# First weights issued after the images, position table and its five products moved behind the patch work

## The reference

```python
patches = x.reshape(B, C, h, P, w, P).transpose(0, 2, 4, 3, 5, 1).reshape(B, h * w, P * P * C)
y = _layernorm(patches, ln1_w, ln1_b)
y = jnp.einsum('bnp,pd->bnd', y, lin_w) + lin_b
y = _layernorm(y, ln2_w, ln2_b)
cls = jnp.broadcast_to(cls_token, (B, 1, y.shape[-1]))
y = jnp.concatenate([cls, y], axis=1)
y = y + pos_embedding[:, :n + 1]
```

## Time and profile before

| | |
|---|---|
| median of 3 runs | 350.81 us (349.03 to 353.78) |
| profiled execution, its own time | 349.38 us |
| its span, first to last instruction | 347.6 us |
| PE busy | 264.2 us (76%) |
| DVE busy | 221.0 us (64%) |
| ACT busy | 113.9 us (33%) |
| POOL busy | 75.7 us (22%) |
| DMA moved | 12.10 MB |

### The profile page before, as it was taken

The page is one execution under the profiler, slowest core; times in us unless marked ns, Lnnn a source line. Parts: engine busy times, 40 slices in busy tenths (PEclk is TensorE's granted clock), DMA queues, the critical chain, the costliest instruction groups (busy, mean ns, idle before and its releaser), DMA issues.

```text
span 347.6 us, 5644 instructions
## 1 busy us (share of the span) xinstructions
PE 264.2 (76%) x2202; PEld 215.6 (62%) x2202; DVE 221.0 (64%) x493; ACT 113.9 (33%) x249; POOL 75.7 (22%) x114
## 2 busy tenths in 40 slices
PE   2078986986695999999996877777585799707397
PEld 2067875986684578777785657556474576407385
DVE  0785577218646488979881258958847346898851
ACT  0034031202421510111133957466231244975000
POOL 5140022012502000000012197929201000333000
PEclk9999995965698999999999999999898599956789
DMA  7930008930000000000000000000000000000001
GB/s 185 298 51 23 2 0 305 307 119 2 2 2 1 2 0 2 0 0 0 3 0 0 3 0 3 2 0 2 3 0 2 0 0 2 0 0 1 0 26 46
DMA packets 16148, 12.10 MB, mean 35 GB/s; under 512 B 4603, under 2 KB 15578, under 8 KB 16122
## 3 DMA queue, kind: packets, MB, share of 16 engines
q1 hardware_dynamic: 13864, 10.01, 10.4%
q10 hardware_dynamic: 2258, 1.73, 1.5%
HBM read 11.13 MB, written 0.61 MB: 34 GB/s over the span
## 4 chain that ended last, share of the span: by engine, by line
PE 50%; DVE 20%; POOL 13%; ACT 7%; DMA 5%; issue 4%; ACTq 0%; DVEq 0%; POOLq 0%
PE bank L1425 37%; POOL big L548 11%; DMA sqr<-in_L_tok_ln_b 5%; DVE part L1318 3%; PE bank L1515 3%; PE bank L1693 2%; PE bank L1420 2%; PE bank L1497 2%; POOL rstd L523 2%; PE bank L1560 2%; DVE big L1381 1%; DVE st L902 1%; PE bank L1577 1%; PE bank L1546 1%; ACT big L635 1%
## 5 line engine op out<-in xcount | busy, mean ns | idle before, releaser
L1425 PE MATMUL bank<-xT,big 128*128 128x296 f32 x160 | 41.4, 413 | 0.0
L1425 PEld LDWEIGHTS bank<-xT,big 128*128 128x128 f32 x160 | 30.3, 190 | 9.2
L548 POOL TENSOR_SCALAR big<-keys_n,k_w 128x256 f32<-128x256 f32 x40 | 30.0, 768 | 23.0 <-DVE keys_n L1047 13.9
L1420 PE MATMUL bank<-ident,ones 128*128 128x128 f32 x128 | 22.9, 353 | 6.3 <-POOL queries_n L516 6.3
L1425 PE MATMUL bank<-xT,fT 128*128 128x296 f32 x96 | 26.0, 431 | 0.3 <-ACT xT L657 0.3
L1318 DVE TENSOR_REDUCE part<-big 128x1 f32<-128x296 f32 (+1 forms) x30 | 18.2, 641 | 12.7 <-ACT big L840 12.5
L1420 PEld LDWEIGHTS bank<-ident,ones 128*128 128x128 f32 x128 | 21.4, 260 | 7.2 <-POOL queries_n L516 6.3
L1425 PE MATMUL bank<-big,cur 128*128 128x256 f32 (+1 forms) x100 | 23.3, 381 | 0.7 <-DVE cur L1159 0.7
L746 ACT ACTIVATE cen<-bank 128x296 f32<-128x296 f32 x20 | 8.3, 417 | 46.4 <-PE bank L1425 40.7
L1425 PEld LDWEIGHTS bank<-xT,fT 128*128 128x128 f32 x96 | 18.9, 200 | 6.6 <-issue 0.8
L523 POOL TENSOR_TENSOR rstd<-var,nhalf 128x5 f32<-128x5 f32 (+3 forms) x7 | 6.8, 976 | 71.8 <-DVE var L913 34.3
(11 more groups left out here) (265 smaller groups left out, 565.6 us busy)
## 6 DMA issues: line engine op xcount, KB each, us to landing
big<-in_x SPq DMA_DIRECT2D x3, 576.0 KB, 9.2
big<-in_L_ffn_w_gate SPq DMA_DIRECT2D x2, 512.0 KB, 9.6
big<-in_L_ffn_w_up SPq DMA_DIRECT2D x2, 512.0 KB, 9.2
big<-in_L_ffn_w_down SPq DMA_DIRECT2D x1, 1024.0 KB, 8.5
big<-in_L_tok_lin_w SPq DMA_DIRECT2D x3, 256.0 KB, 9.5
small<-in_L_ffn_w_gate SPq DMA_DIRECT2D x1, 768.0 KB, 4.6
small<-in_L_ffn_w_up SPq DMA_DIRECT2D x1, 768.0 KB, 6.6
small<-in_L_ffn_w_down SPq DMA_DIRECT2D x1, 768.0 KB, 7.9
```

Source lines behind the costliest of these rows:

```text
L548: ins = pool.tensor_scalar(dst[:, :, n, :], src, scale[:, n:n + 1], by, ALU.mult, ALU.mult)
L1420: pe.matmul(b[:, 0:P], ones[:, :], ident[:, :], start=True, stop=True)
L1425: ins = pe.matmul(out_, a_, b_, start=(n == 0), stop=(n == len(pairs) - 1))
```

## The change

Three moves. On ACT the fourteen weight DMAs wait until all three images have landed. On DVE `make_table` runs behind the normalised patches and no longer between the variance and the wait for the inverse root. On PE, in the list of banks and on ACT, the five `ad` tiles come after the twelve `xp` tiles, and the four dummy products that stood ahead of them are gone.

```diff
@@ fills()
-    for t in range(TT):
-        f.append((("ad", t), "act"))
     for g in range(2):
         for k in range(6):
             f.append((("xp", k, g), "act" if k % 2 else "dve"))
+    for t in range(TT):
+        f.append((("ad", t), "act"))
@@ act
+            for c in range(NC):
+                act.wait_ge(images_in[c], 16)
             for name, arg in (("q0", "L0_attn_Wq"), ("o0", "L0_attn_Wo"), ("q1", "L1_attn_Wq"),
...
-            for t in range(TT):
-                n = P if t < TT - 1 else LAST
-                b = take(act, ("ad", t))
-                empty(act.copy(addend[0:n, t, :], b[0:n, 0:D + 1]))
             act.wait_ge(cols_in, 16 * N_COLS)
...  (the odd xp tiles)
+            for t in range(TT):
+                n = P if t < TT - 1 else LAST
+                b = take(act, ("ad", t))
+                empty(act.copy(addend[0:n, t, :], b[0:n, 0:D + 1]))
@@ dve
-            variance_given(dve.tensor_scalar(var[0:96, 0:NG], mv[0:96, :, 1], EPS, None, ALU.add), make_table)
+            variance_given(dve.tensor_scalar(var[0:96, 0:NG], mv[0:96, :, 1], EPS, None, ALU.add))
...  (normalised patches)
-            dve.wait_ge(consts_ready, N_CONSTS)
+            make_table()
@@ pe
-            for t in range(TT):
-                rows = P if t < TT - 1 else LAST
-                b = fill(("ad", t))
-                if t == 0:
-                    keep_awake(b, 4)
-                    pe.wait_ge(table_ready, 1)
-                full(product(b[0:rows, 0:D + 1], [(sel[:, t * P:t * P + rows], table)]))
...  (the xp transposes)
+            for t in range(TT):
+                rows = P if t < TT - 1 else LAST
+                b = fill(("ad", t))
+                if t == 0:
+                    pe.wait_ge(table_ready, 1)
+                full(product(b[0:rows, 0:D + 1], [(sel[:, t * P:t * P + rows], table)]))
```

## The result

The changed kernel takes 353.13 us (median of 20 runs, 350.55 to 358.36) against 351.97 us for the kernel before in the same session (346.52 to 356.42). The ratio is **1.0103**, 95% interval 1.0067 to 1.0139: about 3.6 us slower. Ratios here are taken over the executions within 1.5% of their own kernel's fastest, nine of the 20 before and 15 of the 20 after; by the means over all 20 (354.00 and 351.54 us) it would be 1.007, 2.5 us. The direction is the same either way, the size is not sharp. The forecast was 353.0 us, +3.3 us in the sum.

The account below looks back on a forecast made before the run. The prediction took the tokenizer's chain up to the projection's first tile as what counts; weights at 0, a projection start 1.2 us later and its slow pace summed to +3.3 us, forecast 353.0 us, range 348.8 to 357.0.

Parts of the forecast that it names:

- The sum: Tokenizer: the projection's first tile `y0` complete at 40.8 us against 37.53, everything behind it moving equally: +3.3 us.
- Weights behind the images, costed at 0: ACT's weight DMAs: waiting for the images gains nothing, with 2.1 us as the upper bound.
- `cols_in` left at 25.4: SP's column loads: the same work, so DVE's small tensors still wait for them until 25.4 us.
- The rival of late columns: SP's column loads slowed by the weights beside them: `cols_in` at 30.5, +8.4 us, 357.8 us; chance 7%.
- Patches 1.5 us earlier: DVE: patches start at 17.5 instead of 19.04 us, with the table following from 22.9 to 24.4.
- Pause, twelve transposes, products on the path: PE: waits until 27.0, twelve transposes to 29.0, five products to 33.3; projection starts 1.2 us later.
- A slow start of the projection: PE's first projection tile: 4.3 us at the slow pace, then 3.2 us for the rest, complete at 40.8.
- The first rival: PE speeds up before the projection, at 31.3 us; `y0` complete at 37.7, +0.2 us, 349.6 us; chance 18%.
- The clock behind the tokenizer, taken as one microsecond either way: Rest of the kernel: the clock it meets, shifted by 3 us, and run spread add a microsecond on either side.

Follow-up runs that it names:

- the two groups of five: Five profiles with the table first, five with products behind the transposes and PE's pause left empty; `y0` read on average at 37.5 and 40.8 us.
- Keeping the pace up: Changed kernel with nine dummy products at the inverse root and ten more ahead of the eighth transposed tile; ratio 0.998 to the kernel before.

## Why the prediction was right

The sum holds: +3.3 us was forecast, and the first tile comes 3.53 us later in the pair of traces, 3.3 us later on average over the two groups of five. Both of its parts hold too: the projection starts 1.1 us later (1.2 forecast), and its first tile takes 2.5 us longer (2.1 forecast). That 353.13 stands beside 353.0 is partly luck. The forecast was built on a profiled execution of 349.38 us; the kernel before had a median of 351.97 in the session of the result, and from there the same sum gives 355.3. The medians are only 1.2 us apart, the means 2.5, the ratio says 3.6. Point by point:

- **Weights behind the images, costed at 0: right.** The statistics end at 15.0 with and without, and with the weights alone moved `y0` came 0.3 us earlier in one profile and 1.1 in the other, within what the kernel before does by itself (36.38 to 39.72 in three profiles up to there). The prediction's byte count took what ran from 9 to 13 us beside the last 0.1 MB of the images for "other loads"; 0.89 of those 1.23 MB were in SP's own queue, where `lin_w` stands behind the images, and only 0.35 in ACT's. The Trainium skill ("DMA: Bandwidth & Descriptors", "Queues, rings and completion order") says that an engine takes turns between queues with work. From that the prediction worked out that the images should come up to 2.1 us earlier; they did not. It doesn't speak against the rule, since ACT's queue moved only 0.05 MB in the first 9 us, and no run here tests it further. The issues of the weights took 7.2 us (12.92 to 20.13), less than the 8.2 to 11.6 assumed, since none stalled.
- **`cols_in` left at 25.4: nearly.** It came at 24.98, with the weights alone at 24.85, without their move at 24.80. The rival of late columns finds no support in these.
- **Patches 1.5 us earlier: right, 17.41.** But fifteen writes took 5.77 us, not the 5.35 they took in the earlier trace rows: the table now follows at 23.10 and not 22.9.
- **Pause, twelve transposes, products on the path: right.** Transposes again from 26.48 (27.0 forecast), products from 28.59 (29.0), projection from 33.17 (33.3). Taking the products away moved the start to 29.59.
- **A slow start of the projection: right, its length mis-sized.** I took 4.3 us; it was 5.1 in the change, 2.9 in the version without the weights' move and 6.2 with the products behind the tile. In the change 0.8 us more at the slow pace is 0.4 us more for the tile (7.9 us instead of 7.5); the projection started 0.1 us earlier than forecast, and the sum is 0.2 us off. Keeping the pace up gave back 5.6 us.
- **The first rival** (PE fast before the projection) fell as the row said it would: neither the 37-row products nor the patch transposes raised the pace. Full transposes of 128 x 128 did, but there are none here.
- **The clock behind the tokenizer, taken as one microsecond either way: wrong in size.** The same kernel, the one with the weights alone moved, took 306.8 and 315.9 us from `y0` to the end in its two profiles. The median of 20 executions stayed in the range; a single one (358.36) did not.

## What to carry to other kernels

When products move behind a wait, ask what kept TensorE at its pace there: work that cost little beside another engine costs twice on the path if it also arrives at the slow pace (4.65 us for the five products here, 2.43 at the fast one). Here dummy work helped when it ended where the real work began and filled the pause in between; at the start of the list it ran at 6.3 us and did nothing for the transposes at 21.2. Judge an edit of a few microseconds by the position of its own landmark in the trace, and time a kernel against itself before believing a ratio of 1%.

## What the runs showed of the hardware

Nine full-height products (3.8 to 4.2 us, in four profiles) or 22 full transposes (4.35 us, in one) brought PE to its fast pace. Nine products of 37 rows (4.2 us) did not, nor did the patch transposes straight behind them. In the two profiles in which 24 fast transposes were followed by an empty pause of 2.75 us, the granted clock fell to 0.50 for 10.2 us, while PE worked without a break on 37-row and then on full products. In the three in which dummy products filled that pause, it stayed at 1.00 through the projection. The length of a pause alone doesn't tell: one of 1.57 us ahead of the projection was followed by no fall in the first profile of the kernel before, one of 1.45 us in its second profile was. And two executions of one kernel, alike up to the first attention but for shifts of about 1 us, were 8.4 us apart at the end. From the first tile on it is 9.1 us, 8.4 of them in three stretches in which the granted clock differed.
